# The context stage of a gated cross-attention block: x loads and quantised rows one chunk later

## What is computed

```
x = x + tanh(g_xattn[0]) * fake_quant(layernorm(x)) @ fake_quant(ctx)   # 8 bit, zero point
x = x + tanh(g_ffn[0])   * (quant_per_token(layernorm(x)) @ W0.T + bias) # W0 = W_int * block scales
x = x + tanh(g_xattn[1]) * attention(layernorm(x), ctx, ctx) @ Wo        # 32 heads, 8 kv heads
x = x + tanh(g_ffn[1])   * layernorm(x) @ W1.T                           # W1 = 4-bit codes * scales
```

## Time and profile before

| | us |
|---|---|
| Median of 3 runs (lowest to highest) | 858.91 (858.64 to 860.24) |
| The profiled execution | 859.74 |
| Its span, first to last instruction | 857.9 |
| PE busy in it | 826.9 |

### The profile page before, as it was taken

The page is one execution under the profiler, slowest core; times in us unless marked ns, Lnnn a source line. Parts: engine busy times, 40 slices in busy tenths (PEclk is TensorE's granted clock), DMA queues, the critical chain, the costliest instruction groups (busy, mean ns, idle before and its releaser), DMA issues.

```text
span 857.9 us, 14034 instructions
## 1 busy us (share of the span) xinstructions
PE 826.9 (96%) x4498; PEld 333.9 (39%) x4498; DVE 589.9 (69%) x850; ACT 448.3 (52%) x741; POOL 535.6 (62%) x235
## 2 busy tenths in 40 slices
PE   8799899899999999999999999999999989999998
PEld 7467644344444432222222222222222213444443
DVE  6886848988488557888888888888888500455622
ACT  4445445555322147777777777777777772111200
POOL 6455329966442417888889888888988886211200
PEclk9989999999999989999999999999999999999999
DMA  7999943336995213554464455456454334122341
GB/s 251 308 241 265 210 150 106 97 86 117 238 228 167 92 59 84 106 127 108 109 133 104 107 103 126 95 125 132 101 113 99 81 68 99 23 52 49 60 137 73
DMA packets 120822, 107.81 MB, mean 126 GB/s; under 512 B 85324, under 2 KB 105804, under 8 KB 116684
## 3 DMA queue, kind: packets, MB, share of 16 engines
q1 hardware_dynamic: 115120, 71.59, 32.1%
q0 software_dynamic: 4608, 33.56, 19.4%
q10 hardware_dynamic: 1052, 2.10, 0.8%
HBM read 41.55 MB, written 12.58 MB: 63 GB/s over the span
## 4 chain that ended last, share of the span: by engine, by line
PE 65%; POOL 10%; issue 7%; DMA 7%; POOLq 3%; DVE 3%; ACT 2%; DVEq 1%; ACTq 0%
PE sbank L1670 10%; PE sbank L1661 9%; PE mpair L1601 9%; POOL wraw L599 6%; DMA tail<-wraw 5%; POOLq L493 3%; PE sbank L1471 3%; PE sbank L1472 3%; PE sbank L1473 3%; PE sbank L1737 3%; PE sbank L1741 3%; PE sbank L1752 3%; PE sbank L1754 3%; PE sbank L1739 3%; POOL xT_lo L494 2%
## 5 line engine op out<-in xcount | busy, mean ns | idle before, releaser
L1333 DVE TENSOR_REDUCE mx<-mpair 128x1 f32<-128x1024 f32 x256 | 302.2, 1216 | 64.2 <-PE mpair L1601 63.2
L891 ACT ACTIVATE regC<-sbank 128x512 f32<-128x512 f32 x512 | 278.1, 594 | 107.6 <-PE sbank L1661 105.6
L1661 PE MATMUL sbank<-regD 98*128 98x512 f16 x512 | 179.5, 386 | 7.9 <-ACT regC L891 5.6
L599 POOL TENSOR_TENSOR wraw<-regC 128x2048 f32<-128x2048 f32 x32 | 148.9, 4652 | 28.6 <-DMA tail<-wraw 17.6
L1601 PE MATMUL mpair<-regD 96*128 96x512 f16 x512 | 157.3, 383 | 0.9 <-DVE mx L1333 0.3
L1670 PE MATMUL sbank<-regC,regD 128*32 128x512 f32 x1024 | 137.2, 608 | 1.0 <-ACT regC L891 1.0
L1661 PEld LDWEIGHTS sbank<-regD 98*128 98x128 f16 x512 | 48.7, 97 | 187.2 <-ACT regC L891 145.9
L599 POOL TENSOR_TENSOR regD<-regC 128x2048 f32<-128x2048 f32 x16 | 75.6, 4727 | 19.5 <-ACT regC L891 19.5
L599 POOL TENSOR_TENSOR tail<-regC 128x2048 f32<-128x2048 f32 x16 | 76.8, 4801 | 0.2 <-ACT regC L891 0.2
L1601 PEld LDWEIGHTS mpair<-regD 96*128 96x128 f16 x512 | 48.0, 98 | 55.1 <-DVE mx L1333 13.8
L492 POOL TENSOR_SCALAR xT_lo<-xT_lo,sc 128x1024 f32<-128x1024 f32 x16 | 30.1, 1878 | 43.7 <-DVE X L1001 35.4
(11 more groups left out here) (185 smaller groups left out, 1255.4 us busy)
## 6 DMA issues: line engine op xcount, KB each, us to landing
regD<-wraw POOLq DMA_DIRECT2D x16, 1024.0 KB, 7.0
tail<-wraw POOLq DMA_DIRECT2D x16, 1024.0 KB, 6.9
xT_lo<-in_ctx SPq DMA_DIRECT2D x16, 512.0 KB, 4.7
wraw<-in_L_ffn_W_int SPq DMA_DIRECT2D x8, 512.0 KB, 4.7
X<-in_x SPq DMA_DIRECT2D x4, 1024.0 KB, 7.2
wraw<-in_L_xattn_Wq SPq DMA_DIRECT2D x8, 512.0 KB, 3.7
wraw<-in_L_xattn_Wo SPq DMA_DIRECT2D x8, 512.0 KB, 4.3
regD<-q_hi_scratch SPq DMA_DIRECT2D x32, 128.0 KB, 2.4
```

What stands on the lines that cost most here:

```text
L599: nc.gpsimd.tensor_tensor(p_sum[pr if pr < 3 else 1][:, :, :], probs[:, (2 * pr) % 4, :, :], probs[:, (2 * pr) % 4 + 1, :, :], ALU.add).th ...
L891: nc.scalar.activation(probs[:, kt % 4, h, :], bank[4 + h % 2], ACT.Exp, scale=SCALE).then_inc(s["exp_ok"], 1)
L1333: v.tensor_reduce(mx[m][:, bass.ds(n, 1)] if par is not None else mx[m][:, n:n + 1], slot[:, :, :], AX.XY, ALU.max).then_inc(s["mx_red"], 1)
L1661: pe.matmul(bank[4 + h % 2], kst[par][0:98, kt * P:(kt + 1) * P], qst[par][0:98, h * 512:(h + 1) * 512], start=True, stop=True).then_inc(s ...
```

## The change

x is loaded and normalised one chunk later. Before, pair c belongs to chunk c. After it, chunk 0 has no pair, chunks 1 and 2 have pairs 0 and 1, and the last chunk has pairs 2 and 3. Every pair has a semaphore of its own for its load. In the first chunk tile 8's high and low parts (`turned_high`, `turned_low` of 2 * TB) are taken at its end instead of at the start of chunk 1. SP issues the loads: pair 0 at the end of the first chunk, pairs 1 and 2 behind the last transposes of chunks 1 and 2, ahead of these chunks' x transposes and second weight block, and pair 3 where it was. The load of scale4 goes to the stage's end. Nothing that is computed changes, and no instruction is added or removed but waits.

SP's stream:

```diff
@@ sync, before the chunks
             load_ctx(5)
-            sp.dma_start(X[:, 0:2, :], x_v[:, 0:2, :]).then_inc(x_in[0], 16)
             load_ctx(6)
+            def load_x(p):
+                pair = slice(2 * p, 2 * p + 2)
+                sp.dma_start(X[:, pair, :], x_v[:, pair, :]).then_inc(x_in[p], 16)
@@ sync, for c in range(NCH - 1)
-                if c == 0:
-                    sp.dma_start(X[:, 2:4, :], x_v[:, 2:4, :]).then_inc(x_in[1], 16)
                 ctx_turn(u + 2)
...
-                xt1(2 * c)
-                if c == 1:
-                    sp.dma_start(X[:, 4:6, :], x_v[:, 4:6, :]).then_inc(x_in[1], 16)
-                    sp.dma_start(scale4[:, :, :], scales4.rearrange("(w p) b -> p w b", p=P)).then_inc(s["sc4_in"], 16)
+                if c > 0:
+                    load_x(c)
+                    xt1(2 * c - 2)
                 if u + TB < U:
                     load_ctx(u + TB + 3)
                 after_wd(2 * c + 1)
-                xt1(2 * c + 1)
+                if c == 0:
+                    load_x(0)
+                else:
+                    xt1(2 * c - 1)
@@ sync, last chunk
-            sp.dma_start(X[:, 6:8, :], x_v[:, 6:8, :]).then_inc(s["x_in2"], 16)
+            load_x(NCH - 1)
             store_k(NCH - 2)
             after_wd(6)
             store_v(NCH - 1)
+            xt1(T - 4)
+            xt1(T - 3)
+            after_wd(7)
             xt1(T - 2)
-            after_wd(7)
             xt1(T - 1)
+            sp.dma_start(scale4[:, :, :], scales4.rearrange("(w p) b -> p w b", p=P)).then_inc(s["sc4_in"], 16)
             store_k(NCH - 1)
```

ACT's stream:

```diff
@@ first_chunk
                 ctx_high(TB + 2)
-                ln1_root(0)
                 k_out(0, 1, True)
-                ln1_affine(0)
                 wd_high(1)
                 ctx_high(TB + 3)
-                ln1_out(0)
-                ln1_affine(1)
-                ln1_out(1)
+                turned_high(2 * TB, 6)
@@ chunk(c)
-                turned_high(u, 6)
+                if c > 1:
+                    turned_high(u, 6)
...
-                ln1_root(c)
-                ln1_affine(2 * c)
+                ln1_root(c - 1)
+                ln1_affine(2 * c - 2)
                 v_out(c, 3, False)
                 ctx_high(u + 3)
-                ln1_out(2 * c)
+                ln1_out(2 * c - 2)
                 k_out(c, 0, False)
-                ln1_affine(2 * c + 1)
+                ln1_affine(2 * c - 1)
                 wd_high(2 * c + 1)
-                ln1_out(2 * c + 1)
+                ln1_out(2 * c - 1)
@@ last chunk
             v_out(c, 2, False)
+            ln1_root(c - 1)
+            ln1_affine(T - 4)
             v_out(c, 3, False)
+            ln1_out(T - 4)
+            ln1_affine(T - 3)
+            ln1_out(T - 3)
+            k_out(c, 0, False)
             ln1_root(c)
-            k_out(c, 0, False)
             ln1_affine(T - 2)
             ln1_out(T - 2)
             ln1_affine(T - 1)
```

DVE's stream:

```diff
@@ first_chunk
                 ctx_round(TB + 1)
-                dve.wait_ge(x_in[0], 16)
-                ln1_stats(0)
-                ln1_affine(0)
                 k_low(0, 1)
                 wd_low(1)
                 ctx_low(TB + 3)
+                turned_low(2 * TB, 6)
                 ctx_round(TB + 2)
-                ln1_round(0)
                 wd_scale(2)
-                ln1_round(1)
                 ctx_round(TB + 3)
@@ chunk(c)
-                dve.wait_ge(x_in[1], 16 * c)
-                ln1_stats(c)
-                ln1_affine(c)
+                ln1_stats(c - 1)
+                ln1_affine(c - 1)
...
-                ln1_round(2 * c)
+                ln1_round(2 * c - 2)
...
-                ln1_round(2 * c + 1)
+                ln1_round(2 * c - 1)
@@ last chunk
             wd_scale(T - 1)
-            dve.wait_ge(s["x_in2"], 16)
+            ln1_stats(c - 1)
+            ln1_affine(c - 1)
+            ln1_round(T - 4)
+            ln1_round(T - 3)
+            k_low(c, 0)
             ln1_stats(c)
             ln1_affine(c)
-            k_low(c, 0)
             ln1_round(T - 2)
             ln1_round(T - 1)
```

More of the change, by code:

```diff
@@ L181, in build @@
         names = """pool_gate act_gate small_in wsc_in sc4_in bias_in wkv0 wkv1 wkv2 wkv3
-            cin0 cin1 cin2 cin3 win0 win1 x_in0 x_in1 x_in2 praw_in
+            cin0 cin1 cin2 cin3 win0 win1 x_in0 x_in1 x_in2 x_in3 praw_in
             ident_ok ones_ok small_mm sc_ok zp_ok gates_ok consts_ok bias_ok
@@ L204, in build @@
         win = [s["win0"], s["win1"]]
-        x_in = [s["x_in0"], s["x_in1"]]
+        x_in = [s[f"x_in{i}"] for i in range(4)]
         q_st = [s["q_st0"], s["q_st1"]]
@@ L747, in first_chunk, with chunk @@
                 ctx_high(TB + 2)
-                ln1_root(0)
                 k_out(0, 1, True)
-                ln1_affine(0)
                 wd_high(1)
                 ctx_high(TB + 3)
-                ln1_out(0)
-                ln1_affine(1)
-                ln1_out(1)
-            def chunk(c, first=False):
+                turned_high(2 * TB, 6)
+            def chunk(c):
                 u = TB * (c + 1)
-                turned_high(u, 6)
+                if c > 1:
+                    turned_high(u, 6)
                 ctx_high(u + 1)
-                v_out(c, 0, first)
-                v_out(c, 1, first)
-                v_out(c, 2, first)
+                v_out(c, 0, False)
+                v_out(c, 1, False)
+                v_out(c, 2, False)
                 wd_high(2 * c)
                 ctx_high(u + 2)
-                ln1_root(c)
-                ln1_affine(2 * c)
-                v_out(c, 3, first)
+                ln1_root(c - 1)
+                ln1_affine(2 * c - 2)
+                v_out(c, 3, False)
                 ctx_high(u + 3)
-                ln1_out(2 * c)
-                k_out(c, 0, first)
-                ln1_affine(2 * c + 1)
+                ln1_out(2 * c - 2)
+                k_out(c, 0, False)
+                ln1_affine(2 * c - 1)
                 wd_high(2 * c + 1)
-                ln1_out(2 * c + 1)
-                k_out(c, 1, first)
+                ln1_out(2 * c - 1)
+                k_out(c, 1, False)
             first_chunk()
@@ L1117, in ln1_stats @@
             def ln1_stats(c):
+                dve.wait_ge(x_in[c], 16)
                 stats(2 * c, 2 * c)
@@ L1145, in chunk @@
                 u = TB * (c + 1)
-                turned_low(u, 6)
+                if c > 1:
+                    turned_low(u, 6)
                 ctx_low(u + 1)
```

## The result

The changed kernel is slower: 865.01 us (862.90 to 866.63, 6 runs) against 859.10 us (858.18 to 861.81, 6 runs); ratio 1.0054, interval 1.0039 to 1.0070. (The recorded ratio is not the quotient of these two medians, which is 1.0069; the loss is 4.6 us by the one and 5.9 by the other.) The profiled execution took 866.63 us, the longest of the six, so what its trace shows is at the upper end.

What follows compares the result with a forecast made beforehand. PE, busy 826.9 of 857.9 us, bounds the kernel. First residual product +1.1 us and clock +2.4 give a 3.5 us shift: span 861.4, median 862.4 us, range 856.5 to 866.5.

Steps and rivals of the forecast that it cites:

- First chunk: Pair 0's layernorm leaves; PE's waits of 4.51 and 1.82 us go, 2.9 us of clock return, PE 9.2 us earlier.
- Chunk 1: Pair 0's statistics wait for x until 51.5, 6.1 us earlier than before (bounds 5.3 to 7.1); net gain 6.2 us.
- The wait forecast at tile 12: In chunk 1, PE waits 3.2 us near 65 before turning context tile 12; the old wait was 0.26.
- Chunk 2: DVE's 5.00 us wait for weight block 5 repeats; pair 1's statistics come at 79.8, 6.6 us earlier.
- The 3.35 before block 6's turn: PE's wait for weight block 6's scaling on DVE, claimed to stay at 3.35 us, with PE resuming at 94.8.
- Last chunk: Two pairs 13.0 us apart delay the first residual product to 126.75; PE idles 7.6 us, clock costs 2.4.
- Behind it nothing changes: After the wait at 164.15, which hands on 3.5 us, the rest of the kernel runs as before.
- The load was not hidden: Rival, last chunk: pair 2's load delays block 7 by only 0.45 us; same time, 859.5 us; chance 0.15.
- The gain of the stage did not survive: Rival: block 5 no longer late, wait below 1 us, PE hardly idles; 4.2 us faster, 854.7; chance 0.15.
- The late x: Rival: first x lands at 53 and block 7 costs 4.4; shift 6.8 us, 865.7 us; chance 0.10.
- DVE and POOL fell alike: Rival, behind the context stage: shifted port conflicts between DVE and POOL, up to 6 us faster or 2 slower; chance 0.08.
- The rule of the page: Evidence against the forecast: closing PE's gap by the skill's advice would make the change right, bringing 4.5 us and more.

Runs made afterwards that it cites:

- e4: Changed kernel with 150 useless small products on PE ahead of the first residual product; ratio to the kernel before 1.0098.
- e1: Changed kernel with the loads of x at their old places, the work on them still one chunk later; ratio to the kernel before 1.0046.
- e2: Changed kernel with weight block 7 issued ahead of pair 2's load; ratio to the kernel before 1.0034.
- e3: Changed kernel with ACT's four copies of the context sums ahead of pair 3's work; ratio to the kernel before 1.0128.
- e5: Changed kernel with context sums, last weight block and key block's last part ahead of pair 3 on ACT, DVE reordered; ratio to the kernel before 1.0066.
- e6: Kernel before with weight block 1 and the key block's second part ahead of pair 0's layernorm in the first chunk; ratio 1.0027.
- e11: Kernel before with pair 0 last in the first chunk, behind weight block 1, tile 8's parts and weight block 2's scaling; ratio 1.0035.
- e10: Changed kernel with pair 2's layernorm cut to 8 of 1024 columns, so wrongly computed; ratio to the kernel before 0.9973.

## Why the prediction was right

"Slower", with 862.4 us in a range of 856.5 to 866.5, was right, and the mechanism with it. The size was short: 6.9 us of span where 3.5 were forecast, and 865.01 us as the median where 862.4 was.

**First chunk.** As forecast: no wait at the turn of tile 8 (38.04, forecast near 38.4), full clock, DVE's low part of block 1 at 35.98 (36.1), PE at the turn behind tile 8's at 44.15 (44.5).

**Chunk 1.** Statistics of pair 0 wait for x, at 53.24 where 51.5 was forecast, outside the bounds given (50.5 to 52.3). The load, issued at 44.19 (45.1 forecast), took 9.0 us where I took 6.4 between bounds of 3.6 and 7.2. This is the first mis-sized term, +1.7: a median of four loads was used as an upper end. It was no accident of one execution, for the nine profiles with the load at this place have 8.4 to 9.8 us. DVE was late by itself as well: it was free at 51.83, not at 50.5, since block 3's load took 6.2 us instead of 4.7 and its scaling 1.89 instead of 1.1. The wait forecast at tile 12 (3.2 us near 65.3) came as 5.55 us, ending at 67.21.

**Chunk 2.** Block 5's wait did not repeat as one wait of 5 us (1.78 before its scaling), since DVE came later (the load itself took longer, 8.8 us against 6.9), but the scaling came at 80.58, 27.3 us behind the statistics of pair 0, as worked out (27.2). The 3.35 before block 6's turn fell to 0.35, and this the prediction had wrong: it let PE keep full clock behind the wait at tile 12. The wait cost clock there:

```profile
66.30:73.20 6.90, 5.99 (x29) 4.73 (x30) 6.81 (x9) 3.75 (x7) 3.08 (x4) 0.51 0.98 248
```

From the turn of tile 12 to that of block 6 PE's own work took 29.2 us instead of 26.5. It cost nothing, because it filled a wait for DVE.

**Last chunk.** Block 7's scaling stands 23.2 us behind pair 1's statistics, forecast 22.0: the second mis-sized term, +1.2. The megabyte ahead of the block cost 3.8 instead of 2.6 us, still inside the bounds (0.45 to 4.4). In the five other profiles with this order the distance is 22.1 to 22.7 us, so 0.5 to 1.1 of the 1.2 belong to this execution and not to the kernel. The ratio goes the same way: its 4.6 us are less than the span's 6.9. The pairs are 12.87 apart (13.0), the copies 9.96 behind (9.65). All together: 1.7 + 0.1 + 1.2 - 0.1 + 0.3 = 3.2 us, and with some 0.2 of latency a0 stands at 130.21 instead of 126.75. The wait is 9.02 (7.6), its clock 2.15 (2.4, inside 1.7 to 3.4); e4 says that without it the key block would have taken back half. "Behind it nothing changes" holds to 0.6 us: the kernel is 6.65 late at a1, 6.61 at the wait behind it and 7.2 at the last query product; the span is 6.9 longer because attention began with a dip of the clock that was 1.5 us shorter and lost most of that again later.

**The rivals.** The load was not hidden (e1, e2). The gain of the stage did not survive: DVE did wait for block 5 by only 1.78 us, but because DVE was late itself, and 5.61 us stood before block 7. The late x (53 and 4.4, shift 6.8) is nearly what happened: 53.2, 3.8 and 6.65. It had 0.10; it should have had more. Its two terms did not come together, though: x was slow in all nine profiles (8.4 us or more), while the megabyte ahead of block 7 cost 2.7 to 3.8 us in the six with that order, never 4.4. DVE and POOL fell alike behind the stage (handed-on shift 6.65, then 6.61), so that rival was not in play in the change, but the same conflict, ahead of a0, decided e3 and e5.

**The rule of the page.** The Trainium skill, Perfetto Trace Analysis, section Identifying Performance Opportunities, has one find the gap and let what blocks it start sooner. In this case that closes the gap (4.51 to none) and loses 6.9 us of span: e6 and e11 show the idleness reappearing at a later turn, and e10 what the moved work costs where it was put.

## What to carry to other kernels

Work taken out of a gap has a second price: where it lands, ask what other work lies beside it and count the whole chain to the first product that needs its end. A median of four like loads is no upper bound: the four of the kernel before took 5.6, 6.6, 7.7 and 9.2 us, and the slowest of them was the fair price for the first one here. Take a mark from several profiles before a shift of 1 us is explained. Before an order is changed so that one engine gets its input early, look at which other engine the same event releases, and compare kernels a few tenths of a per cent apart by marks in the trace as well as by medians.

## What the runs showed of the hardware

- While POOL added two 128x1024 f32 tiles in SBUF (2.3 us each), DVE steps of 128x2 values took 1.2 to 2.2 us instead of 0.16, each until the end of one add; a rounding of 128x1024 f32 took 1.62 to 2.85 instead of 0.69. Reciprocals (0.15) and statistics (1.29) were not slower. Holding POOL back 4 us was worth 4.9 us.
- A program whose order is fixed showed two clocks at one place: 0.66 and 0.76 granted in the 7 us from the table load for attention's exponentials, in two profiles of the kernel before. Over all 14 profiles it was 0.63 to 0.66, 0.76 or 1.00, for 26.4, 24.9 or 23.3 us of the same work.
- One issue can hold SP for long. In the changed kernel the issue of one transpose took 4.72 us (the shortest transpose of the context took 1.23):

```profile
90.40 4.72 SPq L257 DMA_TRANSPOSE regC<-X  x1
...
96.53 0.58 SPq L316 DMA_DIRECT2D X<-in_x  x1
98.43 0.60 SPq L249 DMA_DIRECT2D wraw<-in_L_ffn_W_int  x1
```

The loads of pair 2 and of weight block 7 stand behind it in SP's order. Why that issue is long, and what it alone costs them, was not tried.

- A load of 1 MB of x took 5.5 to 9.8 us from issue to landing over the 14 profiles. Up to 100 us the DMA engines were busy 97 to 98% of the time in both kernels.
